# The first two attentions of a decoder kernel in one straight pipeline: scores in four 32-row groups, softmax a turn ahead of its transposes, a smaller key matrix

## What is computed

```python
# A, per batch
q, k, v = split(x @ W_in.T + b_in)
weights = softmax(where(causal, -inf, q @ k.T * 16 ** -0.5))     # per head
x = layernorm(x + (weights @ v) @ W_out.T + b_out)
# B, per batch
sup, ref = relu(ctx @ W_fc.T + b_fc), relu(x @ W_fc.T + b_fc)
p = softmax((ref @ W_q.T + b_q) @ (sup @ W_k.T + b_k).T * 16 ** -0.5)   # per head
x = layernorm(x + ref + concat(p @ sup @ Wv) + b_v)
```

## Time and profile before

| | before |
|---|---|
| median of 3 runs | 1164.45 us |
| the profiled execution | 1164.86 us |
| its span, first to last instruction | 1163.0 us |
| TensorE matmuls busy | 1030.0 us (89%) |
| VectorE busy | 664.5 us (57%) |
| ScalarE busy | 403.6 us (35%) |
| POOL busy | 331.5 us (29%) |
| mean granted TensorE clock | 0.949 |

### The profile page before, as it was taken

How to read it: one execution, slowest core, us unless ns; L and a number is a source line. 1 busy time by engine, 2 the same in 40 slices (tenths; PEclk the granted TensorE clock), 3 DMA queues, 4 the chain that set the end, 5 groups by cost and what they waited for, 6 DMA issues and landing times.

```text
span 1163.0 us, 18374 instructions
## 1 busy us (share of the span) xinstructions
PE 1030.0 (89%) x5995; PEld 799.9 (69%) x6004; DVE 664.5 (57%) x1043; ACT 403.6 (35%) x748; POOL 331.5 (29%) x556
## 2 busy tenths in 40 slices
PE   4898999858799999999999959967999997599995
PEld 3666766546688888888888834556777875388884
DVE  2777777743355555555555646744556562455555
ACT  1444444522222323322233222322455454133231
POOL 0122222251334344443434430110011002234341
PEclk9999999958899999999999988978999999699998
DMA  7000000006543333333333000001111101364421
GB/s 276 1 1 0 1 1 0 1 1 164 163 135 123 115 114 108 118 105 115 110 118 105 10 8 1 1 21 26 33 30 24 28 18 56 64 168 115 106 50 36
DMA packets 37378, 77.60 MB, mean 67 GB/s; under 512 B 6844, under 2 KB 17888, under 8 KB 36938
## 3 DMA queue, kind: packets, MB, share of 16 engines
q1 hardware_dynamic: 37046, 76.80, 22.6%
q0 software_dynamic: 288, 0.23, 0.2%
HBM read 69.83 MB, written 2.40 MB: 62 GB/s over the span
## 4 chain that ended last, share of the span: by engine, by line
PE 77%; DVE 7%; SPq 6%; ACT 3%; issue 3%; DMA 2%; POOL 1%; ACTq 0%; POOLq 0%; DVEq 0%
PE ps L932 28%; PE ps L943 14%; PE ps L503 5%; PE ps L445 4%; PE ps L613 3%; SPq L346 3%; PE ps L452 2%; SPq L398 2%; PE ps L822 2%; PE ps L514 2%; PE ps L528 2%; PE ps L706 1%; PE ps L757 1%; PE ps L801 1%; PE ps L797 1%
## 5 line engine op out<-in xcount | busy, mean ns | idle before, releaser
L932 PE MATMUL ps<-shared 128*128 128x512 f32 x1560 | 382.4, 395 | 6.0 <-POOL shared L1787 6.0
L932 PEld LDWEIGHTS ps<-shared 128*128 128x128 f32 x1560 | 298.0, 191 | 69.5 <-issue 6.4
L1255 ACT ACTIVATE shared<-pT 128x512 fp32r<-128x512 f32 x130 | 82.2, 632 | 307.6 <-DVE pT L1618 307.6
L1785 POOL CAST shared<-wraw 128x512 fp32r<-128x512 f32 (+1 forms) x130 | 91.6, 705 | 330.1 <-PE ps L943 293.0
L943 PE MATMUL ps<-shared 128*128 128x512 f32 x520 | 162.7, 394 | 11.6 <-DVE al L1621 11.5
L1614 DVE TENSOR_TENSOR e<-e,ps 128x512 f32<-128x512 f32 x130 | 89.3, 687 | 140.4 <-PE ps L932 134.0
L1621 DVE TENSOR_TENSOR al<-pT,shared 128x512 fp32r<-128x512 f32 x130 | 117.2, 902 | 90.8 <-ACT shared L1255 90.8
L1787 POOL TENSOR_TENSOR shared<-wraw,shared 128x512 fp32r<-128x512 f32 (+1 forms) x130 | 132.1, 1016 | 10.4
L1675 POOL TENSOR_SCALAR newton<-agg 128x1 f32<-128x1 f32 (+1 forms) x36 | 8.9, 249 | 416.2 <-DVE agg L1291 389.7
L943 PEld LDWEIGHTS ps<-shared 128*128 128x128 f32 x520 | 98.5, 190 | 34.0 <-DVE al L1621 13.2
L1618 DVE TENSOR_TENSOR pT<-e,kbd 128x512 f32<-128x512 f32 x130 | 100.4, 772 | 24.0 <-DMA kbd<-combine_C 9.6
(11 more groups left out here) (208 smaller groups left out, 1460.2 us busy)
## 6 DMA issues: line engine op xcount, KB each, us to landing
kbd<-combine_C SPq DMA_DIRECT2D x48, 512.0 KB
wraw<-in_C_w SPq DMA_DIRECT2D x48, 384.0 KB, 8.1
kbd<-combine_F SPq DMA_DIRECT2D x17, 512.0 KB
wraw<-in_F_w SPq DMA_DIRECT2D x17, 384.0 KB, 6.8
kbd<-kbd SPq DMA_DIRECT2D x96, 32.0 KB, 1.9
kT<-kbd SPq DMA_DIRECT2D x48, 32.0 KB, 1.8
c_x_t<-in_x_t SPq DMA_DIRECT2D x1, 1024.0 KB, 4.7
c_x_rows<-in_x_rows SPq DMA_DIRECT2D x1, 1024.0 KB, 7.0
```

What stands on the lines that cost most here:

```text
L932: mm = pe.matmul(GU[t][s], w[u][:, (c * 2 + s) * P:(c * 2 + s + 1) * P], xx[:, c, t * HALF:(t + 1) * HALF], start=(i == 0), stop=(i == 5))
L1255: act.activation(ah[t][:, :], a2[t], ACT.Copy).then_inc(S("ah"), 1)
L1785: pool.tensor_copy(wh[u][:, lo:hi], wraw[k][:, lo:hi]).then_inc(S("m_wh"), 1)
```

## The change

One pipeline over 16 items (A's batches 0 to 7, then B's) replaces the two loops. It is straight code of 20 to 22 turns, and in turn t item t is projected, item t-1 scored and exponentiated, item t-2 transposed, copied and multiplied with the values, item t-3 turned to rows and normalized, item t-4 projected and added, items t-5 and t-6 written to XT.

- The 128 features of a chunk are four groups of 32 rows, two heads each. The key matrix k2 holds a chunk's keys only twice, masked to the even or the odd head of the group (128x256 per chunk). Scores are eight matmuls per item with 32 rows and 256 columns, group r at rows 32r into bank r; a unit is now banks 0 and 1, or 2 and 3. In A four masks are written first, one per bank.
- Projections go to the banks PT, which the transposes use too, and B's first products (context) to OB, which the values use.
- x is projected from XT and CTXT directly; VectorE writes the normalized rows to X directly. xs, cs, xn and POOL's copies go.
- All logits of the router stand behind the last x_T.
- The semaphores are counted anew; before_done waits for xn instead of xrow.

```diff
-        xs = [sb(f"xs{u}", [P, C, P]) for u in range(2)]
-        cs = [sb(f"cs{u}", [P, C, P]) for u in range(2)]
-        refT = [sb(f"refT{u}", [P, C, P]) for u in range(2)]
+        refT = [sb(f"refT{u}", [P, C, P]) for u in range(4)]
...
+        k2 = [m[:, 0, 0:2 * C, :].rearrange("p (c s) k -> p c s k", c=C) for m in kbd]
...
-        xb = sb("xb", [P, D])
+        xb = [sb(f"xb{u}", [P, D]) for u in range(2)]
...
-        xn = [sb(f"xn{u}", [P, D]) for u in range(2)]
...
-        SLOT = [ps[:, 2 * s:2 * s + 2, :] for s in range(2)]
+        SC = ps[:, 0:4, :].rearrange("p r (c s k) -> p r c s k", c=C, s=2)
...
+        def item(t):
+            return ("A", t) if 0 <= t < B else ("B", t - B) if B <= t < 2 * B else (None, None)
...
+        def pe_self_cross(pe):
+            def context(i):
+                L, b = item(i)
+                if i == B:
+                    loaded(pe, "B")
+                pe.wait_ge(S("xt"), nb("A", b + 2))
+                pe.wait_ge(S("ot"), i - 2)
+                pe_T(pe, OB[:, 0:D], W["B", "wfc"], XT[:, :, tok(b)])
+                pe_T(pe, OB[:, D:2 * D], W["B", "wfc"], CTXT[:, :, tok(b)]).then_inc(S("fcps"), 1)
+            def project(i):
+                L, b = item(i)
+                if i > 1:
+                    pe.wait_ge(S("pc"), 4 * i - 4)
+                if i == 1:
+                    pe.wait_ge(S("v"), 1)
                 if L == "A":
+                    q_, k_, v_ = XT[:, :, tok(b)], XT[:, :, tok(b)], XT[:, :, tok(b)]
+                else:
+                    pe.wait_ge(S("fc"), 4 * b + 4)
+                    q_, k_, v_ = refT[i % 4], supT[i % 2], supT[i % 2]
+                pe_T(pe, PT[0][:, 0:D], W[L, "wq"], q_)
+                pe_T(pe, PT[0][:, D:2 * D], W[L, "wk"], k_).then_inc(S("qkps"), 1)
+                pe_rows(pe, PT[1][:, 0:D], W[L, "wv"], v_).then_inc(S("vps"), 1)
+            def scores(i):
+                L, b = item(i)
+                if i == 0:
+                    loaded(pe, "A2")
+                pe.wait_ge(S("q"), 2 * i + 2)
+                pe.wait_ge(S("kb"), 4 * i + 4)
+                if i > 0:
+                    pe.wait_ge(S("sub"), 2 * i)
                 if L == "A":
+                    for r in range(4):
+                        pe.matmul(ps[:, r, :], ident16[:, :], causal[:, :], start=True, stop=False, skip_group_check=True)
+                for c in range(C):
+                    for r in range(4):
+                        lo = slice(32 * r, 32 * r + 32)
+                        mm = pe.matmul(ps[:, r, c * D:(c + 1) * D], qT[i % 2][lo, c, :], k2[i % 2][lo, c],
+                                       start=(L == "B"), stop=True, tile_position=(32 * r, 0), skip_group_check=True)
+                mm.then_inc(S("sps"), 1)
+            def transposes(i, u):
+                pe.wait_ge(S("exp"), 2 * i + u + 1)
+                if u == 0:
+                    pe.wait_ge(S("q"), 2 * min(i + 2, 2 * B))
+                    pe.wait_ge(S("kb"), 4 * min(i + 2, 2 * B))
+                    pe.wait_ge(S("v"), min(i + 2, 2 * B))
                 else:
+                    pe.wait_ge(S("pc"), 4 * i + 2)
                 for h in range(2):
                     for q in range(4):
+                        at_ = (h * 4 + q) * P
+                        mm = pe.transpose(PT[h][:, q * P:(q + 1) * P], e[u][:, at_:at_ + P], ident[:, :])
+                    mm.then_inc(S("tr"), 1)
+            def values(i, u):
...
+            def out_rows(i):
+                pe.wait_ge(S("ot"), i + 1)
+                pe.wait_ge(S("z"), i + 1)
                 for k in range(4):
+                    mm = pe.transpose(MB[:, k * P:(k + 1) * P], oT[:, 0, k * P:(k + 1) * P], ident[:, :])
+                mm.then_inc(S("otr"), 1)
+            def out_T(i):
...
+            def out_project(i):
+                pe.wait_ge(S("A_at"), i + 1)
+                if i >= 2:
+                    pe.wait_ge(S("xt"), i)
+                pe_rows(pe, MB[:, D:2 * D], W["A", "wo"], aT).then_inc(S("y"), 1)
+            def ref_rows(i):
+                pe.wait_ge(S("an"), i + 1)
+                pe.wait_ge(S("xt"), i)
                 for k in range(C):
+                    mm = pe.transpose(MB[:, D + k * P:D + (k + 1) * P], refT[i % 4][:, k, :], ident[:, :])
                 mm.then_inc(S("y"), 1)
+            def x_T(i):
+                L, b = item(i)
+                pe.wait_ge(S("xn"), i + 1)
+                pe.wait_ge(S("an"), min(i + 3, 2 * B))
+                pe.wait_ge(S("z"), min(i + 3, 2 * B + 1))
+                pe.wait_ge(S("xt"), i + 1)
                 for k in range(C):
+                    mm = pe.transpose(MB[:, D + k * P:D + (k + 1) * P], X[:, b, k * P:(k + 1) * P], ident[:, :])
                 mm.then_inc(S("xtr"), 1)
+            loaded(pe, "A")
+            for t in range(2 * B + 5):
+                (lp, _), (ls, _), (lv, _), (lo, _), (ly, _), (lx, _) = (item(t - n) for n in range(6))
+                if lv:
+                    transposes(t - 2, 0)
+                if ly == "A":
+                    out_project(t - 4)
+                if ly == "B":
+                    ref_rows(t - 4)
+                if lp == "B":
+                    context(t)
+                if lv:
+                    transposes(t - 2, 1)
+                if ls:
+                    scores(t - 1)
+                if lo:
+                    out_rows(t - 3)
+                if lp:
+                    project(t)
+                if lv:
+                    values(t - 2, 0)
+                    values(t - 2, 1)
+                if lx:
+                    x_T(t - 5)
+                if lo == "A":
+                    out_T(t - 3)
+            pe_logits(pe, "B", range(B))
...
+        def act_self_cross(act):
+            def context(i):
+                L, b = item(i)
+                act.wait_ge(S("fcps"), b + 1)
+                if b >= 4:
+                    act.wait_ge(S("y"), i - 3)
+                if b >= 2:
+                    act.wait_ge(S("vps"), i - 1)
+                for n, dst in enumerate((refT[i % 4], supT[i % 2])):
                     for c in range(C):
+                        act.activation(dst[:, c, :], OB[:, n * D + c * P:n * D + (c + 1) * P], ACT.Relu,
+                                       bias=W["B", "bfc"][:, c:c + 1]).then_inc(S("fc"), 1)
+            def queries(i):
+                L, b = item(i)
+                act.wait_ge(S("qkps"), i + 1)
+                if i >= 2:
+                    act.wait_ge(S("sps"), i - 1)
                 for c in range(C):
+                    act.activation(qT[i % 2][:, c, :], PT[0][:, c * P:(c + 1) * P], ACT.Identity,
+                                   bias=W[L, "bq"][:, c:c + 1]).then_inc(S("q"), 1)
+            def exps(i, u):
+                act.wait_ge(S("sub"), 2 * i + u + 1)
+                act.activation(e[u][:, :], e[u][:, :], ACT.Exp, scale=0.25).then_inc(S("exp"), 1)
+            def copies(i, u):
+                if i > 0:
+                    act.wait_ge(S("pv"), 2 * i - 1 + u)
+                for h in range(2):
+                    act.wait_ge(S("tr"), 4 * i + 2 * u + h + 1)
+                    act.activation(pT[u][:, h * HALF:(h + 1) * HALF], PT[h], ACT.Copy).then_inc(S("pc"), 1)
+            def outputs(i):
+                act.wait_ge(S("pv"), 2 * i + 2)
+                if i > 0:
+                    act.wait_ge(S("otr"), i)
+                act.activation(oT[:, 0, :], OB, ACT.Copy).then_inc(S("ot"), 1)
+            def out_T(i):
...
+            loaded(act, "A")
+            for t in range(2 * B + 6):
+                (lp, _), (ls, _), (lv, _), (lo, _), (ly, _), _, (lx, bx) = (item(t - n) for n in range(7))
+                if ly == "A":
+                    out_T(t - 4)
+                if lx:
+                    act_x(act, lx, bx, MB[:, D:2 * D])
+                if lo:
+                    outputs(t - 3)
+                if lv:
+                    copies(t - 2, 0)
+                if lp == "B":
+                    if t == B:
+                        loaded(act, "B")
+                    context(t)
+                if lv:
+                    copies(t - 2, 1)
+                if lp:
+                    queries(t)
+                if ls:
+                    exps(t - 1, 0)
+                if ls:
+                    exps(t - 1, 1)
...
+        def dve_self_cross(dve):
+            def keys(i):
+                L, b = item(i)
+                if i % B == 0:
+                    loaded(dve, L)
+                dve.wait_ge(S("q"), 2 * i + 2)
                 for c in range(C):
+                    dve.scalar_tensor_tensor(k2[i % 2][:, c], bc(PT[0][:, D + c * P:D + (c + 1) * P], 1, 2),
                                              W[L, "bk"][:, c:c + 1], bc(hmask[:, :], 2, P), ALU.add, ALU.mult)\
+                       .then_inc(S("kb"), 2)
+            def unit(i, u):
+                if u == 0:
+                    dve.wait_ge(S("sps"), i + 1)
```

(56 more changed lines are left out.)

343 lines of the change are left out of this document (47 added, 296 removed).

## The result

The changed kernel takes **1187.5 us** (median of 4 runs, 1179.2 to 1191.1) against 1164.7 (4 runs, 1162.8 to 1165.3): 1.0189 times as long, 95% interval 1.0134 to 1.0243. I had said 1168.5, range 1147 to 1184. It is slower, by the mechanism that I expected, but by 23 us instead of 4. Its profiled execution took 1188.1 us with a span of 1186.3, and its own runs lie 12 us apart where those of the kernel before lie 3 apart.

A forecast was written before the change was run, and what follows sets the result against it. TensorE bounds the kernel before, narrowly; after the change a ring of waits does. 1164.86 - 16.6 (stage at full clock) + 20.4 (low clock) = 1168.7, stated as 1168.5 us, range 1147 to 1184.

The forecast's parts named there:

- the ring: First two attentions: in-order engines wait on each other in a loop once a turn, 12.7 us in A, 12.4 in B.
- the two lines that close it: ScalarE's copies stand behind exps(t-1, 1); TensorE's scores(t) stand behind transposes(t-1, 1), which wait for those copies.
- the logits: Router logits behind the last x_T: 20 more instructions, about 3 us, costed at nothing because POOL's low part covers them.
- Fill: Start of the two-attention stage, up to the subtract of batch 0's second unit, forecast done at 27.1.
- that is 12.7 us: Full turn of A at full clock: ScalarE 3.08, TensorE 2.97, VectorE 6.52; today 13.33.
- 0.86 + 0.17 + 0.03: Ring terms on TensorE from scores to VectorE's max: scores 0.86, tail 0.17, hop 0.03.
- 185.4 + 20.4: Fifteen rings: 185.4 us at full clock, plus 20.4 for TensorE's low clock.
- the drain: End of the stage after the last ring: 14.9 us from 212.5 to 227.4, low clock counted at nothing.
- the clock, 20.4: TensorE's gaps lower its clock: 1.7 us lost in 12 of 15 rings, +20.4; bounds 0 and 40.
- turns 9 to 11: Rings assumed spared the low clock, as out_project and context both fill part of TensorE's gap.
- rival 1: Clock stays at 1.00 as TensorE is never idle much over 2.4 us: 1148, up to 1155; chance 0.30.
- the forecast gain of 16.6 us: Two-attention stage at full clock ends at 227.4 instead of today's 244.0.

The follow-up runs named there:

- the filled kernel: Changed kernel plus 8 filling matmuls behind transposes(t-2, 0) and 3 behind out_project(t-4) in TensorE's gaps, no wait changed: 1163.5 us, ratio 0.9985 to the kernel before.
- the third v buffer: Changed kernel with three v buffers instead of two, nothing else: 1187.4 us, ratio 1.0212 to the kernel before.
- the moved exponential: Changed kernel with ScalarE's exps(t-1, 1) moved behind copies(t-1, 0) of the next turn: 1132.6 us, ratio 0.9721 to the kernel before.

## Why the prediction was wrong in size and right in kind

**Right:** the ring and the two lines that close it; that TensorE runs dry in it; that the four row groups overlap; that the logits, all at the end, cost next to nothing (0.4 us up to the router's transposes); and that the stage between 280 and 690 us changes by less than 2 (0.9 less). Fill ends at 27.09, predicted 27.1.

**Wrong: the step "that is 12.7 us" (and 12.4 in B), the ring's length at full clock.** Measured 13.17 in B, and 13.82 in the two turns of 146.33 and 160.15, for which I had 12.7. The 0.77 in B are, to 0.01, three terms of the VectorE and TensorE sums: no wait was set for values(t) on the two v buffers (0.38 idle; taken away, 0.46); keys were costed like neighbours of one 256-element form, 0.66, and two take 0.88 to the next free moment; from the start of the scores to max it is 1.22 where I had 0.86 + 0.17 + 0.03. The first is of another kind than the others: a wait of an engine that I had walked through line by line, left out since the code's condition, 2i - 2, looks like the turn before and is the same one.

In sum, the 15 rings lasted 218.9 us against 185.4 + 20.4 = 205.8: 13.1 too little, of which the missing 0.77 in each make 11.6.

**Undersized: the drain, 14.9.** It took 18.6 (245.94 to 264.5). I had let the residual of the last batch follow straight behind one late x_T. But its ref_rows wait for the XT copy of the batch before, whose X waits for POOL's Newton steps, and so on back: the last four copies (253.41, 257.59, 260.65, 264.15) come 3.1 to 4.2 us apart. The second transposes and values stand at low clock besides (8 transposes in 1.75 us), which I had set to nothing. In the filled kernel, where most of that is gone, the drain takes 16.7 (230.22 to 246.95): about half of the 3.7 is the clock, the other half the chain of waits.

**Right in sum, partly by luck: the clock, 20.4.** Ring against the nearest ring of its kind at full clock, here or in the filled kernel (less the filling's 0.65), the falls cost about 20 us in the 15 rings, an estimate from these lengths. The count was 12 of 15, as forecast, but not the same ones. I had spared turns 9 to 11, since the output projection and context() both stand in their gap. The spared rings are those of 146.33, 160.15 and 173.97, turns 10 to 12; turn 9 has both as well, and it was hit (130.86 to 146.33, 15.47). The gaps don't tell them apart: 2.96 us in turns 9, 10 and 11, 2.68 in turn 12, 2.69 in turn 13, which was hit. And with the third v buffer 14 were hit. So my reason for the three is not borne out, and the number may be chance. I had 1.7 us for a ring hit, from low stretches of 3.4 us. Most rings with stretches of that length are 1.0 to 1.6 us longer than the nearest full one of their kind (14.75 to 13.17 in B). Five stretches were about twice as long, as the one from 187.7 to 194.5, and the rings of 84.50, 187.14 and 217.62 are 2.2 to 2.7 longer for them, since context() or the projection and the transposes all fall inside.

**Missed: 3.3 us behind 690 (2.4 with the 0.9 won before it).** I had said that stages behind 260 us would change by no more than 2; the third attention met a longer stretch of low clock. Why it begins and ends where it does in each kernel wasn't tried, and as the twelve traces spread over 8.6 us behind that point, these 2.4 may be nothing but chance.

Summed: 13.1 (rings) + 3.7 (drain) + 0.4 (router) + 2.4 (behind it) = 19.6, and 1188.1 less 1168.5 is 19.6. My rival 1, that the clock stays up, is met by the filled kernel, 1163.5 and not 1148: even there the forecast gain of 16.6 us was not to be had. Its stage ends 19.5 us later than my 227.4, of which the ring's missing 0.77 makes 11.6, the filling about 2.6 and the drain 1.8.

## What to carry to other kernels

Before costing a new order of work, walk round the ring once for every engine with all its waits, buffer conditions included, each index written out for the turn in which it is met; and ask of every operation in it who stands behind it in its queue. The cheapest fix was there: an exponential put one place later, behind copies that others waited for, gave 55 us. And where TensorE has gaps, judge an edit with the clock in view, by rings at full clock and not by the time alone: as long as the clock falls in most rings, which ones it hits can hide a saving of half a microsecond in each, as with the third v buffer.

## What the runs showed of the hardware

- In an idle time of 2.69 us (185.92 to 188.61) the granted clock fell to 0.50 at 187.7 and stayed there until 194.5, though TensorE was busy 5.39 of the 6.00 us from 188 to 194. In the prediction's rows an idle 3.15 us was followed by 3.4 us at 0.50. But 2.68 us up to 175.44, and 2.96 up to 148.07 and up to 161.90, were followed by 1.00: the length of the gap alone doesn't say whether the clock falls.
- With the gaps filled to 0.96 us in B and at most 1.23 in A the clock stayed at 1.00 from 47 to 222 us, at equal order and waits; with the moved exponential, at gaps of up to 1.46 us, from 48 to 186.
- Four row groups of 32 rows at 256 columns fp32: 1.15 us for sixteen instructions, against 3.72 in one group and 3.62 over 128 rows; two of 64 rows at 512 columns: 1.13 for four instructions.
- VectorE's subtraction of two SBUF tensors took 4.45 us beside POOL's 4.50 us operation on two SBUF tensors, both ending within 0.6 us of each other, and 0.81 us once that operation had ended, with the last 0.3 us of a smaller one of its kind (1.27 us) and a cast on POOL beside it.
